# Cross attention of a decoder block on one Trainium2 core: heads taken one unit at a time, or two

## Chip, cores, metric

The kernel runs on one core of one Trainium2 chip. The metric is device time in microseconds (us), median of several executions; lower is better. TensorE (PE in the profile) multiplies into PSUM, VectorE is DVE, ScalarE is ACT, GpSimd is POOL, and SyncE (SP) starts DMAs. Each engine runs its own instructions in the order in which they are written, and semaphores order the engines against each other.

## What is computed

A decoder block over 64 batches of 128 tokens with 128 features: linear attention, cross attention and a mixture of experts, each with a residual and a layer norm. The change is in the cross attention, where the queries come from the latents (the result of the first stage) and keys and values from 120 context rows and the 128 latents together. Cut to what matters:

```
lat = layer_norm(latents); xn = layer_norm(context)
q = lat @ Wq                                   # 16 heads of 64
k, v = split(concat([xn, lat]) @ Wkv)          # 248 keys and values
attn = softmax(q @ k.T / 8)                    # per head, 128 x 248
out = (attn @ v).merge_heads() @ Wout
x = layer_norm(latents + out)
```

## The kernel before

Three stages follow each other: linear_attention (to about 285 us of the span), cross_attention (to about 1,697 us) and experts. `cross_attention` goes through 32 rounds r of two batches. A round has 8 pairs of heads j and 2 batches u, so 16 units s = 2j + u; a unit is two heads of one batch.

The operations of TensorE, with the short names that the text uses (after the PSUM tile that they fill):

- T, four transpositions of a unit's probabilities into `ps_T` (two banks; line 1358). It waits for `prob_ready` of its unit.
- S, the scores of the unit LEAD = 3 ahead, two heads of three matmuls each, into `ps_S` (three banks; `scores`, line 1305, by `split_product`, lines 846 to 848). Three matmuls stand for one product because each operand is split into a high and a low part.
- G, `make_G` (line 1294) into `ps_G`, the folded queries of a pair three pairs ahead: six matmuls, in even units.
- V, `make_V` (line 1301) into `ps_V`, a quarter of the values of a half round ahead: three matmuls, in odd units.
- O, `gang_output` (line 1333), 32 matmuls of probabilities by values for four units, into `ps_O`, in units 4, 8, 12 and, for the round before, 0.
- Once a round: `output` (32 matmuls by Wout into `ps_V`, unit 2), `ranks` (unit 2), `keys` (four transpositions into `ps_V`, unit 4), `slots.turn_rows` (unit 10) and `slots.logits` (unit 11). The last two, with `ranks`, serve the routing for the experts.

A unit's softmax goes through four engines. DVE takes the maxima of the scores (`maxima`, line 1170), ACT the exponentials and their sums (`exponentials`, line 1104, two heads), DVE the reciprocals (`inverse`, line 1176), POOL multiplies (`weights`, line 1026), and then PE may transpose; ACT copies the transposition to SBUF (line 1118) for O.

PSUM tiles with one buffer tie the rest: `ps_V` is used by V, `output` and `keys` in turn. V after `output` waits for `sum_ready`, which DVE raises in `residual` (line 1182) when it has read the bank. V after `keys` waits for `kT_ready`, raised by DVE's `keys` (lines 1140 and 1141). `out_copy` (line 1166) empties `ps_O` and `V_copy` (line 1162) empties `ps_V` after V. `G_hi` (ACT, line 1098) and `G_lo` (DVE, line 1156) read `ps_G`. DVE also has the steps of the routing (`slots.route`), small instructions each of which waits for the one before it, at the units that the tables ROUTE (steps 0 to 16) and ROUTE_LATE (steps 17 to 25) name.

The order on each engine is written out by hand in its `body(r, par)`: for TensorE at line 1342, DVE 1191, ACT 1107, POOL 1029. Before, all four go unit by unit:

```
for s in range(UNITS):
    pe.wait_ge(prob_ready, unit + s + 1)      # T of unit s
    scores((unit + s + LEAD) % BANKS, ...)    # S of unit s + 3
```

## Time and profile before

| what | us |
|---|---|
| median of 3 executions (lowest, highest) | 2102.3 (2101.9, 2102.84) |
| the profiled execution: its time | 2103.97 |
| its span | 2102.1 |
| granted TensorE clock, mean over the span | 0.974 of full speed |
| TensorE busy in the span | 1959.1 (93%) |
| DVE, ACT, POOL busy | 1527.5 (73%), 1259.2 (60%), 1338.7 (64%) |

The span is what the rows of the profile lie in; the time of that execution is 1.9 us longer. Durations come from this one execution. A timeline row has its start, its duration and its operation; matmuls are pipelined, so what one costs in a dense stream is the distance from its start to the next one's start, not its duration.

### The profile page before, as it was taken

What the parts mean: (1) busy time and instruction counts of PE and PEld (TensorE: products, weight loads), DVE (VectorE), ACT (ScalarE), POOL (GpSimd) and SP (SyncE); (2) the same over time, 40 slices, a digit from 0 to 9 for tenths busy, and PEclk for the clock granted to TensorE, in tenths of its full rate; (3) what the DMA queues carried; (4) which work ended last, traced back from release to release, by engine and by line L of the source; (5) the groups of instructions that cost most, each with busy time, mean ns of one, the idle gap of its engine ahead of it and who ended that gap; (6) DMA issues with size and microseconds to landing.
All of it is one profiled execution on the core that took longest, in us unless ns stands there. A gap on an engine that the chain in (4) does not pass through costs nothing. (4 is left out here: it accounts for less than half of the span.)

```text
span 2102.1 us, 47412 instructions
## 1 busy us (share of the span) xinstructions
PE 1959.1 (93%) x15991; PEld 1697.7 (81%) x15991; DVE 1527.5 (73%) x4030; ACT 1259.2 (60%) x3812; POOL 1338.7 (64%) x1475
## 2 busy tenths in 40 slices
PE   6888859999999999999999999999999989999874
PEld 4555448999999999999999999998999877888763
DVE  5999946777777777777777777778777755555554
ACT  4565526666666666666666666666666644444453
POOL 5899937566666666666666666666666664444564
PEclk9999969999999999999999999999999999999976
DMA  5200000000000000000000000001000022322344
GB/s 141 58 18 18 16 25 6 9 14 22 16 17 14 22 15 17 15 18 17 18 15 14 21 17 15 15 21 33 19 15 14 21 60 75 85 73 74 96 141 120
DMA packets 105022, 75.78 MB, mean 36 GB/s; under 512 B 11044, under 2 KB 98676, under 8 KB 104660
## 3 DMA queue, kind: packets, MB, share of 16 engines
q1 hardware_dynamic: 93732, 53.66, 9.4%
q0 software_dynamic: 8640, 17.97, 2.5%
q8 instruction: 135, 2.21, 0.5%
q10 hardware_dynamic: 2416, 1.12, 0.2%
q14 instruction: 99, 0.81, 0.1%
HBM read 40.15 MB, written 32.57 MB: 35 GB/s over the span
## 5 line engine op out<-in xcount | busy, mean ns | idle before, releaser
L1026 POOL TENSOR_TENSOR x_prob<-x_prob,x_inv 128x496 f32<-128x496 f32 x514 | 521.8, 1015 | 464.2 <-DVE x_inv L1176 461.7
L1104 ACT ACTIVATE x_prob<-x_ps_S,x_nmax 128x248 f32<-128x248 f32 x1028 | 472.8, 467 | 225.7 <-DVE x_nmax L1170 223.8
L1170 DVE TENSOR_REDUCE x_nmax<-x_ps_S 128x2 f32<-128x496 f32 x515 | 345.0, 670 | 106.0 <-PE x_ps_S L848 98.2
L1118 ACT COPY x_probT<-x_ps_T 124x512 f32<-124x512 f32 x512 | 300.3, 587 | 166.8 <-PE x_ps_T L1358 164.2
L846 PE MATMUL x_ps_S<-x_kT_lo,x_G_hi 128*128 128x248 f32 x1030 | 328.9, 319 | 0.0
L1358 PE MATMUL x_ps_T<-ident,x_prob 128*124 128x128 f32 x2048 | 319.4, 278 | 7.8 <-POOL x_prob L1026 6.3
L1358 PEld LDWEIGHTS x_ps_T<-ident,x_prob 128*124 128x124 f32 x2048 | 233.5, 140 | 74.0 <-POOL x_prob L1026 30.0
L848 PE MATMUL x_ps_S<-x_kT_hi,x_G_hi 128*128 128x248 f32 x1030 | 286.1, 278 | 0.0
L847 PE MATMUL x_ps_S<-x_kT_hi,x_G_lo 128*128 128x248 f32 x1030 | 286.0, 278 | 0.0
L1328 PE MATMUL x_ps_O<-x_probT,x_V 124*64 124x128 f32 x4096 | 251.9, 276 | 0.4 <-ACT x_probT L1118 0.4
L1585 POOL DMA_INDIRECT sorted_results<-e_y,w_wkv x142 | 145.1, 1022 | 164.9 <-DVE e_y L1717 153.4
L1156 DVE TENSOR_TENSOR x_G_lo<-x_ps_G,x_G_hi 128x512 fp32r<-128x512 f32 x259 | 178.0, 687 | 89.5 <-ACT x_G_hi L1098 89.2
L1328 PEld LDWEIGHTS x_ps_O<-x_probT,x_V 124*64 124x64 f32 x4096 | 221.0, 137 | 18.8 <-issue 5.2
L1104 ACT ACTIVATION_READ_ACCUMULATOR x_prob<-x_ps_S,x_nmax 128x1 f32 x1028 | 206.9, 201 | 0.0
L1098 ACT CAST x_G_hi<-x_ps_G 128x512 fp32r<-128x512 f32 x259 | 152.4, 589 | 80.4 <-PE x_ps_G L848 79.7
L847 PEld LDWEIGHTS x_ps_S<-x_kT_hi,x_G_lo 128*128 128x128 f32 x1030 | 196.0, 190 | 0.0
L846 PEld LDWEIGHTS x_ps_S<-x_kT_lo,x_G_hi 128*128 128x128 f32 x1030 | 195.1, 189 | 0.0
L848 PEld LDWEIGHTS x_ps_S<-x_kT_hi,x_G_hi 128*128 128x128 f32 x1030 | 194.5, 189 | 0.0
L1162 DVE COPY x_V<-x_ps_V 124x512 f32<-124x512 f32 x259 | 175.5, 678 | 7.6 <-PE x_ps_V L848 7.6
L281 POOL DMA_INDIRECT sorted_rows<-w_rows,slots_slot x128 | 132.1, 1032 | 27.9 <-issue 23.5
L846 PE MATMUL x_ps_G<-x_kT_lo,x_M_hi 128*128 128x256 f32 x518 | 146.1, 282 | 0.4 <-DVE x_G_lo L1156 0.4
L847 PE MATMUL x_ps_G<-x_kT_hi,x_M_lo 128*128 128x256 f32 x518 | 146.3, 282 | 0.0
(239 smaller groups left out, 4478.7 us busy)
## 6 DMA issues: line engine op xcount, KB each, us to landing
w_wkv<-sorted_rows SPq DMA_DIRECT2D x142, 66.0 KB
e_back<-sorted_results SPq DMA_DIRECT2D x28, 256.0 KB, 3.7
x_nk<-latents SPq DMA_DIRECT2D x34, 124.0 KB
latents<-lin_nlat SPq DMA_DIRECT2D x32, 128.0 KB, 1.8
turned_rows<-w_rows SPq DMA_DIRECT2D x32, 128.0 KB, 1.7
w_wq<-turned_rows SPq DMA_DIRECT2D x32, 128.0 KB
out_dram<-e_result SPq DMA_DIRECT2D x16, 256.0 KB, 2.8
x_nk<-in_ctx SPq DMA_DIRECT2D x34, 120.0 KB, 2.3
```

What stands on the lines that cost most here:

```text
L846: nc.tensor.matmul(out, stationary[0], moving[1], start=first, stop=False)
L847: nc.tensor.matmul(out, stationary[1], moving[0], start=False, stop=False)
L848: return nc.tensor.matmul(out, stationary[0], moving[0], start=False, stop=last)
L1026: nc.gpsimd.tensor_tensor(prob[:, k], prob[:, k], inv[:, k].unsqueeze(2).broadcast_to([P, 2, K]), ALU.mult).then_inc(prob_ready, 1)
L1098: nc.scalar.copy(G_part[0][:, pair], ps_G[:]).then_inc(G_hi_ready, 1)
L1104: nc.scalar.activation(prob[:, k, h, :], ps_S[:, n % BANKS, h * K:(h + 1) * K], ACT.Exp, bias=nmax[:, k, h:h + 1], accum_out=total[:, k, h ...
L1118: nc.scalar.copy(probT[0:KT, s % (2 * GANG)], ps_T[0:KT, s % 2, :]).then_inc(probT_ready, 1)
L1156: nc.vector.tensor_tensor(G_part[1][:, pair].rearrange("p h u q -> p (h u q)"), ps_G[:], G_part[0][:, pair].bitcast(F32).rearrange("p h u ...
L1162: nc.vector.tensor_copy(V[:, hf, u, tile, :], ps_V[0:KT, :]).then_inc(V_ready, 1)
L1170: nc.vector.tensor_reduce(nmax[:, k, :], ps_S[:, n % BANKS, 0:2 * K].rearrange("p (h k) -> p h k", h=2), AX, ALU.max, negate=True).then_in ...
L1328: last = nc.tensor.matmul(ps_O[h * DH:(h + 1) * DH, k * S:(k + 1) * S], V[:, j // 4, u, tile, (j % 4 * 2 + h) * DH:(j % 4 * 2 + h + 1) * D ...
L1358: last = nc.tensor.transpose(ps_T[0:KT, s % 2, at:at + S], prob[:, s % RINGS, h, tile * KT:(tile + 1) * KT], ident[:])
```

## The change

The 16 units of a round become 8 steps of two units on PE, ACT and DVE; POOL's order stays. A step j of TensorE is now: T of both units 2j and 2j+1, S of units 2j+3 and 2j+4, G, whatever falls in that step (`output`, `keys`, `logits`, then O in even steps, then `ranks`), and V last. `turn_rows` stands ahead of step 5. ACT has: both copies of the transpositions, exponentials of unit 2j+3, G_hi, exponentials of unit 2j+4. DVE has: V_copy, the routing steps of the even unit, inverse of unit 2j+2, maxima of units 2j+3 and 2j+4, inverse of unit 2j+3, out_copy, keys or residual, G_lo, the routing steps of the odd unit. The number of instructions that compute stays. Ahead of the first round ACT does the exponentials of three units, before it did two.

The diff: ACT and DVE whole; of TensorE's part the removed lines are left out, the added ones are all there.

```diff
@@ -1106,25 +1106,25 @@

             def body(r, par):
                 unit = r * UNITS
-                for s in range(UNITS):
-                    exponentials(unit + s + 2, (s + 2) % RINGS)
-                    if s == 10 and r:
+                for j in range(PAIRS):
+                    if j == 5 and r:
                         if r == 1:
                             act.wait_ge(part_ready, 10)
                         slots.turned_rows(act, ps_O, r - 1)
-                    if s == 12 and r:
+                    for s in (2 * j, 2 * j + 1):
+                        act.wait_ge(T_psum, unit + s + 1)
+                        nc.scalar.copy(probT[0:KT, s % (2 * GANG)], ps_T[0:KT, s % 2, :]).then_inc(probT_ready, 1)
+                    if j == 6 and r:
                         slots.scores_of(act, r - 1)
-                    act.wait_ge(T_psum, unit + s + 1)
-                    nc.scalar.copy(probT[0:KT, s % (2 * GANG)], ps_T[0:KT, s % 2, :]).then_inc(probT_ready, 1)
-                    if s % 2 == 0:
-                        ahead = s // 2 + 3
-                        G_hi(r * PAIRS + ahead, ahead % 2)
+                    exponentials(unit + 2 * j + 3, (2 * j + 3) % RINGS)
+                    G_hi(r * PAIRS + j + 3, (j + 3) % 2)
+                    exponentials(unit + 2 * j + 4, (2 * j + 4) % RINGS)

             act.wait_ge(wT_psum, 5)
             nc.scalar.copy(gwT[:], ps_O[:, 0:EXPERTS]).then_inc(wT_ready, 1)
             for j in range(3):
                 G_hi(j, j % 2)
-            for k in range(2):
+            for k in range(3):
                 exponentials(k, k)
             rounds(act, body)

@@ -1190,32 +1190,38 @@

             def body(r, par):
                 unit = r * UNITS
-                for s in range(UNITS):
-                    j = s // 2
-                    if s == 0 and later_round(r):
+                for j in range(PAIRS):
+                    s = 2 * j
+                    if j == 0 and r:
                         V_copy(r * 8 + 3, 0, 1, 1)
-                    if s and s % 2 == 0:
+                    if j:
                         k = j - 1
                         V_copy(r * 8 + 4 + k, 1 - k // 4, k % 4 // 2, k % 2)
-                    if s == 5:
+                    routing(r, s)
+                    inverse(unit + s + 2, (s + 2) % RINGS)
+                    maxima(unit + s + 3, (s + 3) % RINGS)
+                    maxima(unit + s + 4, (s + 4) % RINGS)
+                    inverse(unit + s + 3, (s + 3) % RINGS)
+                    if j % 2 == 0 and (j or r):
+                        out_copy(r * GANGS + j // 2 - 1, (j // 2 - 1) % GANGS)
+                    if j == 2:
                         keys(r + 1)
-                    if s % 2:
-                        G_lo(r * PAIRS + j + 3, (j + 3) % 2)
-                    if s % GANG == 1 and (s > 1 or later_round(r)):
-                        out_copy(r * GANGS + s // GANG - 1, (s // GANG - 1) % GANGS)
-                    if s == 3 and later_round(r):
+                    if j == 1 and r:
                         residual(r - 1)
-                    if r and s in ROUTE:
-                        slots.route(dve, ps_O, r - 1, *ROUTE[s])
-                    if r > 1 and s in ROUTE_LATE:
-                        slots.route(dve, ps_O, r - 2, *ROUTE_LATE[s])
-                    if r == MADE:
-                        for k in (s,) if s < 13 else (s * 2 - 13, s * 2 - 12):
-                            slots.table(dve, 0, k)
-                    maxima(unit + s + LEAD, (s + LEAD) % RINGS)
-                    inverse(unit + s + 2, (s + 2) % RINGS)
-                    if s == 7:
+                    G_lo(r * PAIRS + j + 3, (j + 3) % 2)
+                    if j == 3:
                         context_moments(r + 2, par)
+                    routing(r, s + 1)
+
+            def routing(r, s):
+
+                if r and s in ROUTE:
+                    slots.route(dve, ps_O, r - 1, *ROUTE[s])
+                if r > 1 and s in ROUTE_LATE:
+                    slots.route(dve, ps_O, r - 2, *ROUTE_LATE[s])
+                if r == MADE:
+                    for k in (s,) if s < 13 else (s * 2 - 13, s * 2 - 12):
+                        slots.table(dve, 0, k)

             ROUTE = {11: (0, 2), 13: (2, 6), 14: (6, 11), 15: (11, 17)}
             ROUTE_LATE = {3: (RANK_STEP, SLOT_STEP), 6: (SLOT_STEP, 22), 8: (22, STEPS)}
@@ -1341,61 +1347,58 @@

             def body(r, par):
                 unit = r * UNITS
...
+                for j in range(PAIRS):
+                    first = unit + 2 * j
+                    if j == 5 and r:
                         pe.wait_ge(outT_ready, r * GANGS + 2)
                         slots.turn_rows(pe, ps_O, ident, r - 1)
...
+                    for s in (2 * j, 2 * j + 1):
+                        pe.wait_ge(prob_ready, unit + s + 1)
+                        if unit + s > 1:
+                            pe.wait_ge(probT_ready, unit + s - 1)
+                        for h in range(2):
+                            for tile in range(2):
+                                at = (h * 2 + tile) * S
+                                last = nc.tensor.transpose(ps_T[0:KT, s % 2, at:at + S],
+                                                           prob[:, s % RINGS, h, tile * KT:(tile + 1) * KT], ident[:])
+                        last.then_inc(T_psum, 1)
+                    for s in (2 * j, 2 * j + 1):
+                        ahead = (s + LEAD) // 2
+                        if s % 2:
+                            pe.wait_ge(G_lo_ready, r * PAIRS + ahead + 1)
+                        scores((unit + s + LEAD) % BANKS, (s + LEAD) % 2, par if ahead < PAIRS else 1 - par, ahead % 2)
+
+                    ahead = j + 3
+                    pe.wait_ge(G_lo_ready, r * PAIRS + ahead)
+                    if j == 5:
+                        pe.wait_ge(kT_lo_ready, r + 2)
+                    make_G(ahead % 2, par if ahead < PAIRS else 1 - par, ahead % PAIRS)
+                    if j == 1 and r:
                         pe.wait_ge(V_ready, r * 8 + 5)
                         output(r - 1)
...
+                    if j == 2:
                         pe.wait_ge(V_ready, r * 8 + 4 + 2)
                         keys(r + 1, 1 - par)
...
+                    if j == 5 and r:
+                        slots.logits(pe, ps_O, r - 1)
+                    if j % 2 == 0 and first:
+                        if j == 6 and r:
                             pe.wait_ge(slots.shifted_ready, r)
...
+                        if j == 2 and r > 1:
+                            pe.wait_ge(slots.routed, (r - 2) * STEPS + SLOT_STEP)
+                        gang_output(r * GANGS + j // 2 - 1)
+                    if j == 1 and r > 1:
                         pe.wait_ge(outT_ready, r * GANGS)
                         slots.ranks(pe, ps_O, r - 2)
+                    if j == 1 and r:
+                        pe.wait_ge(sum_ready, r)
+                    elif j == 2:
+                        pe.wait_ge(kT_ready, r + 2)
+                    else:
+                        pe.wait_ge(V_ready, r * 8 + 4 + j)
+                    if j == 4:
+                        pe.wait_ge(kT_lo_ready, r + 2)
+                    make_V(par if j < 4 else 1 - par, 1 - j // 4, j % 4 // 2, j % 2)

             pe.wait_ge(kT_lo_ready, 1)
             for k in range(4):
```

How the order moves, at three places. The first is TensorE in a round's steady part, from one T on; a name is out<-in, and what stands in brackets are the semaphores waited for. Before:

```order
L1358 MATMUL x_ps_T<-ident,x_prob 124x128 [waits x_probT_ready,x_prob_ready]
L1358 MATMUL x_ps_T<-ident,x_prob 124x128 x3
L846 MATMUL x_ps_S<-x_kT_lo,x_G_hi 128x248 [waits x_G_lo_ready]
L847 MATMUL x_ps_S<-x_kT_hi,x_G_lo 128x248
L848 MATMUL x_ps_S<-x_kT_hi,x_G_hi 128x248
L846 MATMUL x_ps_S<-x_kT_lo,x_G_hi 128x248
L847 MATMUL x_ps_S<-x_kT_hi,x_G_lo 128x248
L848 MATMUL x_ps_S<-x_kT_hi,x_G_hi 128x248
L846 MATMUL x_ps_V<-x_wv_lo,x_kT_hi 124x512 [waits x_V_ready]
```

And with the change:

```order
L1362 MATMUL x_ps_T<-ident,x_prob 124x128 [waits x_probT_ready,x_prob_ready]
L1362 MATMUL x_ps_T<-ident,x_prob 124x128 x3
L1362 MATMUL x_ps_T<-ident,x_prob 124x128 [waits x_probT_ready,x_prob_ready]
L1362 MATMUL x_ps_T<-ident,x_prob 124x128 x3
L846 MATMUL x_ps_S<-x_kT_lo,x_G_hi 128x248
L847 MATMUL x_ps_S<-x_kT_hi,x_G_lo 128x248
L848 MATMUL x_ps_S<-x_kT_hi,x_G_hi 128x248
L846 MATMUL x_ps_S<-x_kT_lo,x_G_hi 128x248
L847 MATMUL x_ps_S<-x_kT_hi,x_G_lo 128x248
L848 MATMUL x_ps_S<-x_kT_hi,x_G_hi 128x248
L846 MATMUL x_ps_S<-x_kT_lo,x_G_hi 128x248 [waits x_G_lo_ready]
```

Before, one T is followed by one S and then V or G. Now the T of the next unit stands between a T and the S, and both S follow each other.

The second place is DVE around the copy of the new keys (lines 1140 and 1141), step j = 2. Before:

```order
L1162 COPY x_V<-x_ps_V 124x512
L1170 TENSOR_REDUCE x_nmax<-x_ps_S 128x2
L1176 RECIPROCAL x_inv<-x_total 128x2
L1140 TENSOR_SCALAR x_kT_full<-x_ps_V,w_gain 128x2x120
L1141 TENSOR_SCALAR x_kT_full<-x_ps_V,w_gain 128x2x128
L1156 TENSOR_TENSOR x_G_lo<-x_ps_G,x_G_hi 128x512
L1166 COPY x_outT<-x_ps_O 128x512
```

And with the change:

```order
L1162 COPY x_V<-x_ps_V 124x512
L1176 RECIPROCAL x_inv<-x_total 128x2
L1170 TENSOR_REDUCE x_nmax<-x_ps_S 128x2 x2
L1176 RECIPROCAL x_inv<-x_total 128x2
L1166 COPY x_outT<-x_ps_O 128x512
L1140 TENSOR_SCALAR x_kT_full<-x_ps_V,w_gain 128x2x120
L1141 TENSOR_SCALAR x_kT_full<-x_ps_V,w_gain 128x2x128
L1156 TENSOR_TENSOR x_G_lo<-x_ps_G,x_G_hi 128x512
```

The copy of the keys stood ahead of `out_copy` (line 1166), and now stands behind it.

The third place is DVE around routing steps 6 to 10 (lines 373 to 381), from the end of steps 2 to 5 (line 371), in units 13 and 14. Before:

```order
L371 SCALAR_TENSOR_TENSOR slots_order<-slots_equal,slots_index 128x16
L1170 TENSOR_REDUCE x_nmax<-x_ps_S 128x2
L1176 RECIPROCAL x_inv<-x_total 128x2
L1162 COPY x_V<-x_ps_V 124x512
L373 TENSOR_REDUCE slots_col<-slots_order 128x2
L375 TENSOR_TENSOR slots_chosen<-slots_order,slots_col 128x16
L377 SCALAR_TENSOR_TENSOR slots_rest<-slots_chosen,slots_score 128x16
L379 TENSOR_REDUCE slots_col<-slots_rest 128x2
L381 TENSOR_TENSOR slots_equal<-slots_rest,slots_col 128x16
L1170 TENSOR_REDUCE x_nmax<-x_ps_S 128x2
```

And with the change:

```order
L369 TENSOR_TENSOR slots_equal<-slots_score,slots_col 128x16
L371 SCALAR_TENSOR_TENSOR slots_order<-slots_equal,slots_index 128x16
L1162 COPY x_V<-x_ps_V 124x512
L373 TENSOR_REDUCE slots_col<-slots_order 128x2
L375 TENSOR_TENSOR slots_chosen<-slots_order,slots_col 128x16
L377 SCALAR_TENSOR_TENSOR slots_rest<-slots_chosen,slots_score 128x16
L379 TENSOR_REDUCE slots_col<-slots_rest 128x2
L381 TENSOR_TENSOR slots_equal<-slots_rest,slots_col 128x16
L1176 RECIPROCAL x_inv<-x_total 128x2
L1170 TENSOR_REDUCE x_nmax<-x_ps_S 128x2 x2
L1176 RECIPROCAL x_inv<-x_total 128x2
```

Before, the maxima of one unit stood between the two groups of routing steps. Now both groups and `V_copy` stand ahead of an inverse and the next maxima.

## Rows read from the trace of the kernel before

**Rows 1.** The page, its head: the span.

```profile
span 2102.1 us, 47412 instructions
```

**Rows 2.** Windows: us, busy time (x instructions) by engine, clock, DMA share, GB/s.

```profile
500.00:1400.00 900.00, 898.27 (x8502) 826.65 (x8502) 685.80 (x1873) 599.36 (x1894) 586.74 (x695) 1.00 0.06 17
```

**Rows 3.** One line, L1358: ns min/median/max, first and last start, forms.

```profile
L1358 PE MATMUL x_ps_T<-ident,x_prob x2048: 270/272/421, 318.8 to 1686.0; 128*124 128x128 f32 x187
```

**Rows 4.** Timeline, TensorE, 865 to 869 us: start us, us, operation.

```profile
865.67 0.40 PE L846 MATMUL x_ps_V<-x_wv_lo,x_kT_hi 128*124 128x512 f32 x1
...
866.37 0.60 PE L1358 MATMUL x_ps_T<-ident,x_prob 128*124 128x128 f32 x4
...
866.72 0.36 PE L846 MATMUL x_ps_S<-x_kT_lo,x_G_hi 128*128 128x248 f32 x1
...
867.15 0.28 PE L846 MATMUL x_ps_S<-x_kT_lo,x_G_hi 128*128 128x248 f32 x1
...
867.49 0.28 PE L846 MATMUL x_ps_G<-x_kT_lo,x_M_hi 128*128 128x256 f32 x1
...
868.21 0.60 PE L1358 MATMUL x_ps_T<-ident,x_prob 128*124 128x128 f32 x4
```

**Rows 5.** Timeline, all engines, 881 to 908 us: what is read and overwritten.

```profile
881.29 0.26 PE L326 MATMUL x_ps_O<-slots_picked,slots_ones 128*128 128x24 f32 x1
...
881.58 0.42 DVE L1182 TENSOR_TENSOR slots_hsum<-x_ps_V,X 128x256 f32<-128x256 f32 x1 [2.26 <-PE x_ps_V L1317]
...
885.86 0.53 DVE L1140 TENSOR_SCALAR x_kT_full<-x_ps_V,w_gain 128x240 f32<-128x240 f32 x1 [0.40 <-PE x_ps_V L1263]
...
886.31 0.53 DVE L1141 TENSOR_SCALAR x_kT_full<-x_ps_V,w_gain 128x256 f32<-128x256 f32 x1
...
905.33 1.97 PE L1328 MATMUL x_ps_O<-x_probT,x_V 124*64 124x128 f32 x32
...
907.23 0.66 PE L1358 MATMUL x_ps_T<-ident,x_prob 128*124 128x128 f32 x4
...
907.34 0.69 DVE L1166 COPY x_outT<-x_ps_O 128x512 f32<-128x512 f32 x1 [0.60 <-PE x_ps_O L1328]
```

**Rows 6.** Timeline, all engines, 903 to 905 us: the softmax chain of a unit.

```profile
903.40 0.60 PE L1358 MATMUL x_ps_T<-ident,x_prob 128*124 128x128 f32 x4
...
903.72 0.15 DVE L1176 RECIPROCAL x_inv<-x_total 128x2 f32<-128x2 f32 x1
...
903.84 0.47 ACT L1104 ACTIVATE x_prob<-x_ps_S,x_nmax 128x248 f32<-128x248 f32 x1 [0.48 <-DVE x_nmax L1170]
...
903.96 1.01 POOL L1026 TENSOR_TENSOR x_prob<-x_prob,x_inv 128x496 f32<-128x496 f32 x1 [0.97 <-DVE x_inv L1176]
...
904.65 0.20 ACT L1104 ACTIVATION_READ_ACCUMULATOR x_prob<-x_ps_S,x_nmax 128x1 f32 x1
...
904.73 0.67 DVE L1170 TENSOR_REDUCE x_nmax<-x_ps_S 128x2 f32<-128x496 f32 x1 [0.27 <-PE x_ps_S L848]
```

**Rows 7.** Timeline, VectorE, 866 to 869 us and 907 to 909 us: routing steps.

```profile
867.17 0.16 DVE L373 TENSOR_REDUCE slots_col<-slots_order 128x2 f32<-128x16 f32 x1
...
868.33 0.67 DVE L1170 TENSOR_REDUCE x_nmax<-x_ps_S 128x2 f32<-128x496 f32 x1
...
907.95 0.16 DVE L365 TENSOR_REDUCE slots_col<-slots_score 128x2 f32<-128x16 f32 x1
...
908.66 0.67 DVE L1170 TENSOR_REDUCE x_nmax<-x_ps_S 128x2 f32<-128x496 f32 x1
```

**Rows 8.** Windows, other stages, columns as in rows 2.

```profile
96.00:106.00 10.00, 8.37 (x37) 5.22 (x35) 9.93 (x18) 6.06 (x15) 9.28 (x7) 1.00 0.05 13
...
2001.50:2005.00 3.50, 1.29 (x8) 0.94 (x8) 2.81 (x14) 0.63 (x2) 3.02 (x4) 1.00 0.25 55
...
2005.00:2008.50 3.50, 3.35 (x16) 3.02 (x15) 1.46 (x4) 2.79 (x8) 2.01 (x2) 0.53 0.65 198
```

**Rows 9.** Waits, 500 to 1400 us: us in total, times, longest us.

```profile
PEld x_ps_T L1358 <- POOL x_prob L1026: 15.1, 43, 0.5
```

42 lines of the change are left out of this document (removed).

## The prediction

> **What bounds the kernel now.** I read the windows by stage first, because the change touches one stage only. From 500 to 1400 us, inside the cross attention, TensorE is busy for 898.27 of 900 us at the full clock, while DVE has 686, ACT 599 and POOL 587 us [rows 2]. So TensorE sets the pace, and the other three have slack in total. The stage has 512 units; their transpositions start between 318.8 and 1686.0 us [rows 3], so a unit takes 2.67 us and a round of 16 takes 42.7 us. The waits say how near the softmax chain is: T waited for POOL 43 times in those 900 us, for 15.1 us in all, twice a round at the most [rows 9]. The chain reaches TensorE just in time.
>
> **Price of TensorE's stream**, as distances between starts in a dense piece [rows 4]: V 0.70 us (865.67 to 866.37), T 0.35 (to 866.72), S 0.77 (to 867.49), G 0.72 (to 868.21). The second half of S took 0.34 (867.15 to 867.49), so the first half after a T took 0.43: the switch from a transposition to a product costs some 0.08 us. O took 1.90 (905.33 to the T at 907.23), and DVE reads its result from 907.34 on, 0.11 later [rows 5].
>
> **What the change gains.** Before, each of 16 S of a round follows a T; now 8 do. That is 8 x 0.08 = 0.64 us a round. Whatever else changes neighbours (V after O instead of T after O) I take at nothing, as both are a switch out of the same O; bounds are the 0.08 either way, four times a round, 0.3 us.
>
> **What the change costs: the lead of S over T.** Unit 2j+3 gets its scores in step j and its transposition as the second T of step j+1. Between that T and the one of step j TensorE has only one step of work. The loop closes: the second T releases S in program order, S releases the softmax, the softmax releases the second T of the next step. Its length is read in one place [rows 6]:
> - second T starts at 903.40, its S is ready and the maxima start at 904.73: 1.33 us;
> - maxima 0.67;
> - exponentials with their sums from 903.84 to 904.65 + 0.20: 1.01;
> - reciprocal start to POOL's start, 903.72 to 903.96: 0.24;
> - POOL 1.01;
> - three more handovers (DVE to ACT, ACT to DVE, POOL to PE). The one from DVE to POOL took 0.09 (903.72 + 0.15 to 903.96); most are shorter, and I estimate 0.13 for the three.
>
> Sum 4.39 us. A step without O holds S + S + G + V + T + T = 0.77 + 0.69 + 0.72 + 0.70 + 0.35 + 0.35 = 3.58 us; with the switches rounded less coarsely 3.59. Before, the distance was three units, at least 5.5 us, and covered the chain. Now each short step ends in a wait:
> - step 3: 4.39 - 3.59 = 0.80 us.
> - step 5: it also holds the logits, four matmuls like a T, taken as 0.36: 0.44 us left.
> - step 7: here DVE is late besides. After step 6's O (end at time 0) DVE has out_copy from 0.11, occupying it 0.61 (907.34 to 907.95), G_lo the same, routing steps 2 to 5 0.71 (907.95 to 908.66), V_copy 0.61 (as many elements as out_copy), steps 6 to 10 1.16 (867.17 to 868.33), the inverse 0.08 [rows 5, 7]. The next maxima can start at 3.89. Their S is ready 1.33 after a second T that starts at 0.70 + 0.36 = 1.06, so at 2.39. The chain is 1.50 longer: 4.39 + 1.50 - 3.59 = 2.30 us. The third place in the order shows the cause, the maxima no longer stand between the two groups.
> - steps 0, 2, 4, 6 hold an O, 5.5 us and more, and step 1 `output`, 3.5 us: no wait.
>
> **Two waits for `ps_V`.** In step 2, V stands right behind O and waits for `kT_ready`. DVE does `out_copy` first, and that waits for O's end. From O's end: 0.11, then 0.61, then the two key copies, 885.86 to 886.31 + 0.53 = 0.98, and 0.05 to wake PE: 1.75 us idle [rows 5]. Before, T and S stood between, and the copies ran under O. In step 1, V waits for `sum_ready`: the residual's read started 0.29 us after `output` ended (881.29 to 881.58) and took 0.42 [rows 5]; with the wake-up 0.76, of which `ranks` covers 0.22: 0.54 us. Both have the work that used to hide them behind them now.
>
> **turn_rows** in step 5 waits for the `out_copy` of step 4's O, with only V between: 0.11 + 0.69 - 0.70 = 0.1 at least, more where routing steps 22 to 25 delay DVE; I take 0.3 (bounds 0.1 and 0.6).
>
> **Sum.** Costs 0.80 + 0.44 + 2.30 + 1.75 + 0.54 + 0.30 = 6.13; gains 0.64, and 0.4 of present waits that these replace (15.1 us over 21 rounds is 0.7 on the load side, less in the stream). Net 5.1 us a round. Round 0 has no residual, O or routing and waits for POOL's splitting of weights anyway, so 31 rounds: +158 us. Linear attention and experts don't change.
>
> **The clock.** The waits make TensorE idle for about an eighth of a round, and at the turn of the round nearly without a break: T alone lies between some 0.5 and 1.8 us of idle. In the experts' stage a stretch of 3.5 us with 1.29 us of work at full clock was followed by one at 0.53 of it, 1.2 instead of 2.4 GHz, for 3.5 us; a stretch of the first stage with 8.37 of 10 us busy kept 1.00 [rows 8]. The turn of the round is like the former, the rest like the latter. One such fall costs 3.4/2 = 1.7 us. Between never and each round I take one round in three, as how the idle time falls matters: 0.55 us a round, +17 us. The Trainium skill (TensorE: Matmul & The Clock Gate, Why this matters for your kernels) warns only of idle gaps between bursts longer than any single one expected here; by that rule this term is nothing and the time 2260. The rows above, a fall after a gap of 2.2 us, speak for the term.
>
> The profiled execution took 2103.97 us for a span of 2102.1 [rows 1]. 2104 + 158 + 17 = 2279; it stood 1.7 above the median, so **2278 us**, 8% slower.
>
> **Rivals.**
> - *The chain fits.* If the softmax of a unit took under 3.6 us from T to T, and the two V waits were hidden, only the switches would remain: 2102 - 32 x 0.64 = 2082 us, faster. For it: the mean busy shares of 65 to 76% [rows 2]. Against it: the 4.39 us come from engines that did not queue, and nothing in the change shortens them. It decides at 3.6 us. Chance 0.03.
> - *The chain alone.* DVE's late maxima and the V waits could be shorter than worked out, if DVE gets through its queue faster than these rows say, or if the bank is free earlier than the semaphores' order suggests. With the chain's 0.80 + 0.44 + 0.80 alone: 2.04 - 1.04 = 1.0 a round, 2133 us. Chance 0.05.
> - *The clock falls in each round.* 1.7 instead of 0.55 a round: 2314 us; with a second fall at step 2's 1.75 us wait, 2350. For it: the rows of the experts' stage. Against it: in step 2 dense O and V stand on both sides. Chance 0.17.
> - *Nothing moves*, if the slots were taken up elsewhere. The order on TensorE did change in each round. Chance 0.01.
>
> The forecast has 0.74. The range goes from 2215 to 2325. Below: the V waits, turn_rows and DVE's delay a quarter smaller ((1.75 + 0.54 + 0.30 + 1.50) x 0.25 x 31 = 32 us), no fall of the clock (17) and the chain 0.15 shorter at its three places (14). Above: a fall each round and 10 us. This leaves out the rivals at 2082, 2102 and 2133 and the double fall, under 0.2 in all. A change under 0.2% can't be told from none here. Faster by more 0.03, within it 0.01, slower 0.96.
>
> **What would show it.** In the profile after: PE busy near 88% of a longer cross stage, rounds of about 48 us; DVE, ACT and POOL busy the same in us. Among the waits, T for POOL's `x_prob` grows from 15 us to about 4 us a round, V for the keys and for the residual appear new with 1.7 and 0.5 us. S in second place takes 0.69. If the second T of steps 4, 6 and 0 doesn't wait, the chain is misread; if V of step 2 doesn't wait, the order on DVE isn't what decides; a clock of 0.97 over the stage confirms the one in three.

## The result, and the profile after

| | us | runs | ratio to before, 95% interval |
|---|---|---|---|
| before | 2102.1 | 4, 2099.61 to 2102.84 | |
| after | 2297.36 | 4, 2293.72 to 2299.96 | 1.093, 1.0909 to 1.0951 |

The change makes the kernel 9.3% slower. The prediction was 2278 us in a range of 2215 to 2325. The direction and the range hold; the median lies 19 us above the point.

The page of the kernel after: its head (answers to [rows 1]), TensorE's busy time, and the costliest group of the transpositions (busy us, mean ns of one, idle us before them and the releaser of most of it).

```profile
span 2293.2 us, 47416 instructions
...
PE 2009.0 (88%) x15991; PEld 1722.9 (75%) x15991; DVE 1508.6 (66%) x4030; ACT 1253.0 (55%) x3816; POOL 1339.4 (58%) x1475
...
L1362 PE MATMUL x_ps_T<-ident,x_prob 128*124 128x128 f32 x2048 | 289.4, 276 | 85.5 <-POOL x_prob L1026 81.6
...
L846 PE MATMUL x_ps_V<-x_wv_lo,x_kT_hi 128*124 128x512 f32 x260 | 121.7, 468 | 72.6 <-DVE x_kT_full L1141 53.8
```

DVE, ACT and POOL have nearly the same busy time as before (1508.6, 1253.0 and 1339.4 against 1527.5, 1259.2 and 1338.7 us). The span is 191 us longer, and TensorE is idle in 141 of it (2293.2 less 2009.0 is 284, before 143). Two groups, T and V, hold 158 us of the idle time. TensorE's busy time grew as well, by 50 us for the same work: a matmul at half the clock counts as busy, and a short wait can hide under the duration of the matmul ahead of it (more on that at the last experiment).

Windows of the kernel after, columns as in [rows 2]:

```profile
500.00:1500.00 1000.00, 904.48 (x8260) 819.79 (x8261) 652.94 (x1816) 577.15 (x1840) 570.91 (x673) 0.99 0.05 15
```

Before it was 898.27 of 900 us [rows 2]; now it is 90%. By the starts of T, which go from 319.6 to 1876.7 us here against 318.8 to 1686.0 [rows 3], the median round takes 48.46 instead of 42.80 us, 48.43 where the clock stays up and 49.95 where it doesn't. The waits of TensorE in the same 1000 us (20.6 rounds), load side and stream, answer to [rows 9]:

```profile
PEld x_ps_T L1362 <- POOL x_prob L1026: 77.8, 82, 1.9
...
PE x_ps_T L1362 <- POOL x_prob L1026: 51.4, 62, 1.7
...
PE x_ps_V L846 <- DVE x_kT_full L1141: 33.6, 20, 1.7
...
PE x_ps_V L846 <- DVE slots_hsum L1182: 7.9, 20, 0.4
```

T waits on the load side four times a round for 3.8 us, where it waited twice for 0.7. V waits once a round for the keys and once for the residual, both new.

One round in TensorE's timeline, 1011 to 1049 us (start, duration, operation). A new row begins where another operation does; its start minus the one before it is what that operation took.

```profile
1011.51 0.26 PE L328 MATMUL x_ps_O<-slots_picked,slots_before 128*128 128x16 f32 x1
1012.16 0.49 PE L846 MATMUL x_ps_V<-x_wv_lo,x_kT_hi 128*124 128x512 f32 x1 [0.39 <-DVE slots_hsum L1182]
...
1016.44 1.97 PE L1334 MATMUL x_ps_O<-x_probT,x_V 124*64 124x128 f32 x32
1020.09 0.49 PE L846 MATMUL x_ps_V<-x_wv_lo,x_kT_hi 128*124 128x512 f32 x1 [1.68 <-DVE x_kT_full L1141]
...
1020.89 1.04 PE L1362 MATMUL x_ps_T<-ident,x_prob 128*124 128x128 f32 x8
...
1021.68 0.36 PE L846 MATMUL x_ps_S<-x_kT_lo,x_G_hi 128*128 128x248 f32 x1
...
1023.15 0.28 PE L846 MATMUL x_ps_G<-x_kT_lo,x_M_hi 128*128 128x256 f32 x1
...
1024.56 0.60 PE L1362 MATMUL x_ps_T<-ident,x_prob 128*124 128x128 f32 x4
1025.72 0.65 PE L1362 MATMUL x_ps_T<-ident,x_prob 128*124 128x128 f32 x4 [0.56 <-POOL x_prob L1026]
1026.13 0.36 PE L846 MATMUL x_ps_S<-x_kT_lo,x_G_hi 128*128 128x248 f32 x1
...
1030.29 0.50 PE L846 MATMUL x_ps_V<-x_wv_lo,x_kT_hi 128*124 128x512 f32 x1
...
1031.15 0.44 PE L311 MATMUL x_ps_O<-ident,w_rows 128*128 128x128 f32 x2
...
1035.53 1.39 PE L1362 MATMUL x_ps_T<-ident,x_prob 128*124 128x128 f32 x8
1036.67 0.36 PE L846 MATMUL x_ps_S<-x_kT_lo,x_G_hi 128*128 128x248 f32 x1
...
1040.85 0.50 PE L846 MATMUL x_ps_V<-x_wv_lo,x_kT_hi 128*124 128x512 f32 x1
...
1041.64 1.03 PE L1362 MATMUL x_ps_T<-ident,x_prob 128*124 128x128 f32 x8
...
1044.60 0.40 PE L846 MATMUL x_ps_V<-x_wv_lo,x_kT_hi 128*124 128x512 f32 x1
...
1045.68 0.65 PE L1362 MATMUL x_ps_T<-ident,x_prob 128*124 128x128 f32 x4 [0.22 <-POOL x_prob L1026]
...
1048.02 0.66 PE L1362 MATMUL x_ps_T<-ident,x_prob 128*124 128x128 f32 x4 [1.69 <-POOL x_prob L1026]
1048.43 0.36 PE L846 MATMUL x_ps_S<-x_kT_lo,x_G_hi 128*128 128x248 f32 x1
```

Without a wait, two T take 0.79 us (1020.89 to 1021.68). From there each wait of the round can be read off. They stand where the loop closes: what a short step 3, 5 or 7 lacks shows at the T of step 4, 6 or 0. In the 17 rounds from the fourth to the thirtieth that have no fall of the clock, every one of these distances is the same within 0.02 us, except at the turn, where it varies by up to 0.13.

- Behind step 3: two T take 1.57 (1024.56 to 1026.13), 0.78 too long.
- Behind step 5: 1.14 (1035.53 to 1036.67), 0.35 too long.
- Turn of the round: V takes 1.08 up to the first T (1044.60 to 1045.68) instead of 0.70, and the two T take 2.75 (to 1048.43): 0.38 + 1.96 = 2.34.
- V for the keys: O takes 3.65 (1016.44 to 1020.09) instead of 1.90: 1.75.
- V for the residual: 0.65 from the last of `ranks` (1011.51 to 1012.16), against 0.11 in a later version ("`output` first") where it doesn't wait: 0.54.
- `turn_rows`: the V ahead of it takes 0.86 (1030.29 to 1031.15). A V that stands behind an O and is followed by nothing that waits takes 0.79 (1040.85 to 1041.64), so this wait is 0.06.

The turn of the round on DVE and POOL, the same execution:

```profile
1044.28 0.17 DVE L381 TENSOR_TENSOR slots_equal<-slots_rest,slots_col 128x16 f32<-128x16 f32 x1
1044.37 0.16 DVE L1176 RECIPROCAL x_inv<-x_total 128x2 f32<-128x2 f32 x1
1044.45 1.23 DVE L1170 TENSOR_REDUCE x_nmax<-x_ps_S 128x2 f32<-128x496 f32 x2
1046.17 0.17 DVE L1176 RECIPROCAL x_inv<-x_total 128x2 f32<-128x2 f32 x1 [0.49 <-ACT x_prob L1104]
```

```profile
1044.61 1.01 POOL L1026 TENSOR_TENSOR x_prob<-x_prob,x_inv 128x496 f32<-128x496 f32 x1 [3.18 <-DVE x_inv L1176]
...
1045.80 1.12 POOL L281 DMA_INDIRECT sorted_rows<-w_rows,slots_slot  x1 [0.17 <-issue]
1046.95 1.02 POOL L1026 TENSOR_TENSOR x_prob<-x_prob,x_inv 128x496 f32<-128x496 f32 x1
```

The maxima start 3.60 us after O's end (1040.85 to 1044.45), behind the last routing step. The reciprocal is done at 1046.34, but POOL multiplies only at 1046.95, because the scatter of sorted rows (line 281) stands ahead of it. T follows POOL's end at 1048.02.

The clock in two turns of the round, windows of 3.4 us (the clock is the third number from the right):

```profile
995.60:999.00 3.40, 1.59 (x12) 1.36 (x13) 2.42 (x10) 2.69 (x11) 3.03 (x4) 1.00 0.06 20
999.00:1002.40 3.40, 3.40 (x19) 3.18 (x18) 2.09 (x6) 1.51 (x6) 1.81 (x3) 0.50 0.08 25
...
1045.60:1049.00 3.40, 1.63 (x13) 1.39 (x14) 2.42 (x10) 2.69 (x11) 3.03 (x4) 1.00 0.09 25
1049.00:1052.40 3.40, 3.40 (x48) 3.27 (x46) 2.02 (x6) 2.39 (x9) 1.95 (x3) 1.00 0.06 20
```

Both turns have the same pauses. After the one TensorE runs at 0.50, 1.2 GHz, for 3.4 us and gets 19 matmuls done, after the other at 1.00 and gets 48. Such a fall follows 10 of the 31 turns; all ten start 2.7 to 3.4 us behind the first T of a round.

### The profile page after: what moved, and what is told of

It is laid out like the page before. It is cut to its first block and busy times, and to the rows that moved or that the text cites. A ratio compares the mean times of both kernels' runs of the same rounds, so it can differ in the third digit from the quotient of the medians.

```text
span 2293.2 us, 47416 instructions
## 1 busy us (share of the span) xinstructions
PE 2009.0 (88%) x15991; PEld 1722.9 (75%) x15991; DVE 1508.6 (66%) x4030; ACT 1253.0 (55%) x3816; POOL 1339.4 (58%) x1475
## 5 line engine op out<-in xcount | busy, mean ns | idle before, releaser
L1116 ACT COPY x_probT<-x_ps_T 124x512 f32<-124x512 f32 x512 | 287.1, 593 | 367.1 <-PE x_ps_T L1362 365.0
L1170 DVE TENSOR_REDUCE x_nmax<-x_ps_S 128x2 f32<-128x496 f32 x515 | 337.6, 669 | 86.2 <-PE x_ps_S L848 83.1
L1362 PE MATMUL x_ps_T<-ident,x_prob 128*124 128x128 f32 x2048 | 289.4, 276 | 85.5 <-POOL x_prob L1026 81.6
L846 PE MATMUL x_ps_S<-x_kT_lo,x_G_hi 128*128 128x248 f32 x1030 | 312.1, 303 | 0.0
L848 PE MATMUL x_ps_S<-x_kT_hi,x_G_hi 128*128 128x248 f32 x1030 | 291.1, 283 | 0.0
L1104 ACT ACTIVATION_READ_ACCUMULATOR x_prob<-x_ps_S,x_nmax 128x1 f32 x1030 | 214.3, 208 | 0.0
L1166 DVE COPY x_outT<-x_ps_O 128x512 f32<-128x512 f32 x128 | 88.5, 692 | 183.3 <-PE x_ps_O L1334 183.3
L846 PE MATMUL x_ps_V<-x_wv_lo,x_kT_hi 128*124 128x512 f32 x260 | 121.7, 468 | 72.6 <-DVE x_kT_full L1141 53.8
L1176 DVE RECIPROCAL x_inv<-x_total 128x2 f32<-128x2 f32 x514 | 82.4, 160 | 104.6 <-ACT x_prob L1104 104.6
```

The costliest lines, as they stand in the source:

```text
L846: nc.tensor.matmul(out, stationary[0], moving[1], start=first, stop=False)
L848: return nc.tensor.matmul(out, stationary[0], moving[0], start=False, stop=last)
L1104: nc.scalar.activation(prob[:, k, h, :], ps_S[:, n % BANKS, h * K:(h + 1) * K], ACT.Exp, bias=nmax[:, k, h:h + 1], accum_out=total[:, k, h ...
L1116: nc.scalar.copy(probT[0:KT, s % (2 * GANG)], ps_T[0:KT, s % 2, :]).then_inc(probT_ready, 1)
L1170: nc.vector.tensor_reduce(nmax[:, k, :], ps_S[:, n % BANKS, 0:2 * K].rearrange("p (h k) -> p h k", h=2), AX, ALU.max, negate=True).then_in ...
L1362: last = nc.tensor.transpose(ps_T[0:KT, s % 2, at:at + S], prob[:, s % RINGS, h, tile * KT:(tile + 1) * KT], ident[:])
```

## The experiments

All are edits of the kernel after, but the last and "the other engines' alone", which edit the kernel before. The round is the median distance of T over 16 units in the profiled execution; "falls" are the stretches of 3.4 us at 0.50 in the cross attention, without the one within 5 us of the stage's start that most versions have, before too. Edits move lines, so T is at L1356 to L1366 in their rows.

| version | us (runs) | ratio, 95% interval | round | falls |
|---|---|---|---|---|
| after | 2297.36 (4) | 1.0930, 1.0909 to 1.0951 | 48.43 | 10 |
| keys first | 2252.23 (4) | 1.0716, 1.0698 to 1.0734 | 46.68 | 19 |
| routing steps behind the maxima | 2261.33 (4) | 1.0755, 1.0737 to 1.0773 | 47.73 | 1 |
| `output` first | 2266.78 (4) | 1.0791, 1.0773 to 1.0809 | 47.89 | 3 |
| scatter late | 2262.71 (4) | 1.0769, 1.0751 to 1.0787 | 47.92 | 0 |
| T S T S | 2222.33 (4) | 1.0576, 1.0559 to 1.0594 | 46.64 | 0 |
| the four repairs together | 2172.15 (4) | 1.0330, 1.0313 to 1.0347 | 44.91 | 0 |
| TensorE's order alone | 2736.88 (2) | 1.3017, 1.2969 to 1.3066 | 61.56 | 79 |
| the other engines' alone | 2418.91 (2) | 1.1505, 1.1482 to 1.1528 | 52.07 | 17 |
| repairs and T S T S | 2133.90 (5) | 1.0151, 1.0136 to 1.0165 | 43.80 | 0 |
| and V ahead of O | 2187.05 (5) | 1.0405, 1.0391 to 1.0419 | 45.48 | 0 |
| and steps behind G_lo | 2105.55 (11) | 1.0018, 1.0009 to 1.0027 | 42.92 | 0 |
| before, two waits taken away | 2085.55 (5) | 0.9925, 0.9911 to 0.9939 | 42.30 | 0 |

(The rounds of the first, second and ninth line are of those without a fall. Before: 42.80 and none.)

**Keys first.** In step 2 DVE reads the keys ahead of `out_copy`.

```diff
+                    if j == 2:
+                        keys(r + 1)
                     if j % 2 == 0 and (j or r):
                         out_copy(r * GANGS + j // 2 - 1, (j // 2 - 1) % GANGS)
-                    if j == 2:
-                        keys(r + 1)
```

> The changed kernel, with VectorE's copy of the new keys moved ahead of out_copy in step 2. Theory (out_copy between the transposed keys and kT_ready makes V wait 1.75 us a round behind O): the wait of V for the keys goes to nothing, but 0.35 to 0.4 us of it comes back as a longer wait of the second T in step 4, whose chain the pause had covered. Net -1.35 to -1.45 us a round, 31 rounds: 2297 - 43 = about 2253 us. Rival (V waits because O holds TensorE or the bank, whatever VectorE does first): the wait stays, 2297 us.

Measured: the wait of V for the keys is gone, and the round without a fall is 1.75 us shorter (48.43 to 46.68). The term is confirmed to the hundredth. The 0.35 to 0.4 us that were to come back in step 4 did not: the two T there take 1.59 us, before the edit 1.57. That the time came out at the expected 2253 is luck. The time fell by 45 us and not by 54, because 19 instead of 10 rounds have a fall, though the waits at the turn are the same.

**Routing steps behind the maxima.** In step 7 DVE does the maxima and the inverse first, the steps 6 to 10 behind them.

```diff
-                    routing(r, s)
+                    if j < 7:
+                        routing(r, s)
                     inverse(unit + s + 2, (s + 2) % RINGS)
                     maxima(unit + s + 3, (s + 3) % RINGS)
                     maxima(unit + s + 4, (s + 4) % RINGS)
                     inverse(unit + s + 3, (s + 3) % RINGS)
+                    if j == 7:
+                        routing(r, s)
```

> The changed kernel, with routing steps 6 to 10 of step 7 moved behind the two maxima and the inverse on VectorE. Theory (VectorE is late for the maxima in step 7, so T waits 2.3 us at the turn of the round, and that long pause makes the clock fall in one round of three): the wait at the turn shrinks by 1.0 to 1.1 us, the first of the two T does not wait at all, and the granted clock no longer falls at the turn, 15 us more. 2297 - 32 - 15 = about 2250 us. Rival 1 (the wait is the chain's length alone): unchanged, 2297 us. Rival 2 (the clock falls because of the idle share of the whole round, not of that pause): about 2265 us, with still some 8 to 10 stretches at half clock.

Measured: 0.70 us a round, and the falls nearly gone. 0.70 x 31 = 22 us and nine falls of 1.5 us make the 36 us; the expectation had 47. The steps took 0.91 us in the kernel after (1043.46 to 1044.37 on DVE), and the turn did get 0.90 shorter: V takes 0.70 instead of 1.08 and the two T 2.23 instead of 2.75. But 0.19 came back right behind: the two S of step 0 take 1.65 instead of 1.46, because the moved steps now stand ahead of G_lo, for which the second S waits. One of the steps had become long besides:

```profile
1029.71 1.57 DVE L375 TENSOR_TENSOR slots_chosen<-slots_order,slots_col 128x16 f32<-128x16 f32 x1
```

**`output` first.** In step 1 TensorE does `output` ahead of G, so that G covers the read of the residual.

```diff
+                    if j == 1 and r:
+                        pe.wait_ge(V_ready, r * 8 + 5)
+                        output(r - 1)
                     ahead = j + 3
                     pe.wait_ge(G_lo_ready, r * PAIRS + ahead)
...
                     make_G(ahead % 2, par if ahead < PAIRS else 1 - par, ahead % PAIRS)
-                    if j == 1 and r:
-                        pe.wait_ge(V_ready, r * 8 + 5)
-                        output(r - 1)
```

> The changed kernel, with the output product of step 1 ahead of G. Theory (V in step 1 waits 0.54 us because nothing but ranks stands between output and V): G's 0.7 us cover the residual's read, the wait for the sum goes, nothing takes its place: -0.54 us x 31 = -17 us, 2280 us. Rival (VectorE's residual starts late because it stands behind the second inverse): the wait moves with it, 2297 us.

Measured: 0.54 us a round, as the term said, 17 us. Of the other 14 us of the gain, some 10 come with seven falls fewer, which the expectation of 2280 us did not have; the rest is not accounted for. Taking away half a microsecond some 12 us behind the turn changed how often the turn's pauses bring the clock down.

**Scatter late.** Both of POOL's scatters of a round go behind its last multiplication.

```diff
-                    if s > 13 and r > 1:
-                        slots.scatter(pool, r - 2, 0, s - 14)
+                    if s == 15 and r > 1:
+                        for u in range(2):
+                            slots.scatter(pool, r - 2, 0, u)
```

> The changed kernel, with both scatters of a round's end (POOL's indirect DMAs, 1.1 us each) behind POOL's last multiplication of the round instead of one before it and one behind. Theory (at the turn of the round the inverse is done at 1046.34 us of the changed kernel's trace, and POOL starts the multiplication only at 1046.95, when its scatter ends; so 0.5 of the 2.34 us wait there is POOL's): the wait at the turn shrinks by 0.5 us a round, 2297 - 16 = 2281 us, and down to 2266 if the clock then stops falling. Rival (the multiplication would wait for the inverse and its handover anyway): 2297 us.

Measured: 0.51 us a round and no fall left. So POOL's scatter is a part of the wait at the turn, the one read off POOL's timeline above, and not of the prediction's sum.

**T S T S.** Steps, waits and the other engines stay; only the inner order of TensorE changes back.

```diff
                         last.then_inc(T_psum, 1)
-                    for s in (2 * j, 2 * j + 1):
                         ahead = (s + LEAD) // 2
```

> The changed kernel, with TensorE's four groups of a step in turns, T S T S, as before the change; all the rest stays. Theory A (the loop from one second T over the S behind it to the next second T sets the short steps; and the switch from T to S costs nothing, as T T S S took 2.25 us in the trace, the same as 2 x (0.35 + 0.77)): the S of unit 2j+3 is released by the first T, 0.4 us earlier than its own step's second T, so the waits of steps 3 and 5 (0.78 and 0.35 us) go, and the one at the turn shrinks from 2.3 to about 1.6 us; the outT wait before turn_rows grows by 0.6. Net about -1.1 us a round, 2263 us, less up to 15 where the clock no longer falls. Theory B (as the prediction had it, each change from T to S costs 0.08 us): 0.64 us a round dearer than A, 2283 us; T S T S would then be longer than T T S S by 0.16 us in the trace.

Measured: 75 us less, better than either theory. The waits behind steps 3 and 5 vanish (1.13), that at the turn shrinks from 2.34 to 1.64 (V takes 1.07 instead of 0.70, T S T S 3.52 instead of 2.25), and no fall is left; the other three stay. Theory A missed 26 to 41 us, mostly because it had the wait before `turn_rows` grow by 0.6 us: the V ahead of it takes 0.86 us in both versions. TensorE's timeline of this version, a step without a wait:

```profile
1037.03 0.60 PE L1362 MATMUL x_ps_T<-ident,x_prob 128*124 128x128 f32 x4
...
1037.38 0.36 PE L846 MATMUL x_ps_S<-x_kT_lo,x_G_hi 128*128 128x248 f32 x1
...
1038.16 0.60 PE L1362 MATMUL x_ps_T<-ident,x_prob 128*124 128x128 f32 x4
...
1039.28 0.28 PE L846 MATMUL x_ps_G<-x_kT_lo,x_M_hi 128*128 128x256 f32 x1
```

T S T S takes 2.25 us (1037.03 to 1039.28). T T S S in the kernel after takes 2.26 (1020.89 to 1023.15). There are twice as many changes from T to S, and they cost nothing.

**The four repairs together**: the four diffs ahead of T S T S.

> The changed kernel with four repairs at once: keys ahead of out_copy, routing steps 6 to 10 behind the maxima, output ahead of G, both scatters behind the last multiplication. TensorE's order T T S S stays. Theory (what is left is the loop over the second T, with 0.8 us in step 3, 0.45 in step 5, 0.8 at the turn, and V behind O at 0.05 a time): 2.0 + 0.2 - 0.4 = 1.8 us a round over the kernel before, 2102 + 31 x 1.8 = about 2158 us, no falls of the clock. Rival (the repairs overlap: each hides behind a wait that another one takes away): over 2190 us.

Measured: 14 us more than expected, with 44.91 a round, 2.11 above before. The four repairs took 3.5 us off a round, as much as one by one (1.75 + 0.70 + 0.54 + 0.51), so they don't overlap. The timeline accounts for 2.0 of the 2.11 that are left: 0.77 behind step 3 and 0.35 behind step 5, which no repair touches, 0.91 for T and 0.18 for S at the turn, 0.2 for V behind O (below), less the 0.4 that the present waits of before had. The expectation had 1.8; it took the turn's rest at 0.8 where T and S together have 1.09.

**TensorE's order alone** has TensorE's new block with the old ones of ACT and DVE; **the other engines' alone** has ACT's and DVE's new ones with TensorE's old. In the blocks that are new:

```diff
-                for s in range(UNITS):
+                for j in range(PAIRS):
...
```

> TensorE's new order alone; ScalarE and VectorE keep the order by units of the kernel before. Theory (in that order G_hi and G_lo stand between the exponentials and the inverse of the odd unit, and G comes later in TensorE's new step; the loop over the second T is then longer in every step, also in those with O): waits of 1 to 3.6 us for T in seven of eight steps, 16 us more a round: about 2600 us. Rival (the order on ScalarE and VectorE matters little, as both have slack): like the changed kernel without its wait for the keys, 2250 us.

> The new order on ScalarE and VectorE alone; TensorE keeps the order by units of the kernel before. Theory (VectorE then takes two maxima ahead of one inverse and of G_lo, so TensorE's G waits for G_lo, V for the keys and for the residual): 8 to 9 us more a round, about 2370 us. Rival (TensorE's lead of three units covers any order behind it): 2110 to 2150 us.

Measured: each half alone is far worse than both, with two executions each. Waits of the first from 500 to 1400 us (14.6 rounds):

```profile
PE x_ps_T L1356 <- POOL x_prob L1026: 195.3, 114, 3.1
```

and of the second (17 rounds):

```profile
PE x_ps_V L846 <- DVE x_kT_full L1141: 43.6, 17, 2.6
PE x_ps_G L846 <- DVE x_G_lo L1156: 32.8, 85, 0.6
...
PE x_ps_V L846 <- DVE slots_hsum L1182: 24.1, 17, 1.4
```

With TensorE's order alone T waits in each step for a softmax that, by the order as written, the other engines issue one unit late; 79 falls of some 1.5 us are 119 of its 635 us over before. The expectation of 2600 had no falls; without them, its 16 us a round hold. With the others' order alone T hardly waits, but everything that TensorE wants from DVE one unit earlier is late, for 9.3 us a round where 8 to 9 were expected; 17 falls come on top. The matching of the orders, which the change does, saves over 120 us against either half. It isn't what costs.

**Repairs and T S T S**: the four repairs and the edit of T S T S.

> The four repairs together with the turns T S T S on TensorE. Theory (the step by pairs itself costs nothing and gains nothing; all of its loss is the loop over the second T, VectorE's order, output, and POOL's scatter, and V behind O costs 0.05 us more than T behind O): the 1.9 us of waits for T that were left in the run with four repairs (44.9 us a round) go, so 43.0 to 43.3 us a round, 2108 to 2118 us, at par or half a per cent over the kernel before. Rival (fewer switches between T and S did save 0.6 us a round in T T S S, which is given back now): over 2125 us.

Measured: 2133.9, some 20 above, and as high as the rival has it. One wait remained that the expectation hadn't:

```profile
1014.01 1.02 DVE L375 TENSOR_TENSOR slots_chosen<-slots_order,slots_col 128x16 f32<-128x16 f32 x1
...
1015.58 0.68 DVE L1157 TENSOR_TENSOR x_G_lo<-x_ps_G,x_G_hi 128x512 fp32r<-128x512 f32 x1
```

```profile
1015.06 0.65 PE L1366 MATMUL x_ps_T<-ident,x_prob 128*124 128x128 f32 x4
1016.31 0.38 PE L846 MATMUL x_ps_S<-x_kT_lo,x_G_hi 128*128 128x248 f32 x1 [0.60 <-DVE x_G_lo L1157]
```

The routing steps, moved behind the maxima, now stand ahead of G_lo, for which S waits. My own repair had made a new wait; the version with that repair alone had it already, at 0.19 us.

**And V ahead of O**: on top of that version, V goes ahead of O in steps 0, 4 and 6.

```diff
+                    if j in (0, 4, 6):
+                        pe.wait_ge(V_ready, r * 8 + 4 + j)
...
+                        make_V(par if j < 4 else 1 - par, 1 - j // 4, j % 4 // 2, j % 2)
                     if j % 2 == 0 and first:
...
                         gang_output(r * GANGS + j // 2 - 1)
```

> As the run with the repairs and the turns, and V ahead of O in steps 0, 4 and 6. Theory (the first V behind O takes 0.33 instead of 0.23 us, the first T behind O 0.16 instead of 0.11): 0.05 us less, three times a round, 5 us under the run with the turns: 2103 to 2113 us. Rival (the end of O then stands right ahead of T, out_copy later against turn_rows in step 5): back to par with that run.

Measured: 53 us slower than the version that it edits, where 5 us less were expected. V behind O had been the cover for `out_copy`; without it `turn_rows` waits (500 to 1400 us):

```profile
PE x_ps_O L311 <- DVE x_outT L1167: 15.9, 20, 0.8
```

and T waits again at the turn (8.8 us in 19 times). By the order that is because O ends 0.7 us later, and with it `out_copy` and all that stands behind it on DVE; no run takes this apart. The rival named the right mechanism, but not the size: it had this version at par.

**And steps behind G_lo**: on top of the repairs with T S T S.

```diff
-                    if j == 7:
-                        routing(r, s)
...
                     G_lo(r * PAIRS + j + 3, (j + 3) % 2)
+                    if j == 7:
+                        routing(r, s)
```

> The four repairs with the turns, but steps 6 to 10 of the routing chain issued behind G_lo instead of ahead of it. Theory: in the version with them ahead, the scores of the second unit at the turn of the round waited 0.6 us for G_lo (11.9 us over 20 waits), because those small steps, one of them 1.02 us long beside POOL, stood ahead of it; with them behind, that wait goes: 43.8 less 0.6 to 0.9 gives about 43.0 us a round, and 2134 less some 25 gives about 2108 us. Rival: the chain at the turn has its next member right behind (maxima, inverse, POOL), so that another wait takes its place, and the time stays between 2125 and 2134 us.

Measured: 2105.55 us over 11 runs, 42.92 a round, 0.88 less, and no wait of S for G_lo left. The theory holds. It also refutes the rival of the version that it edits: nothing had to be given back for more changes from T to S. With T S T S, the four repairs and this one the new form is back to 0.2% from before, and no faster.

**Before, two waits taken away.** An edit of the kernel before: `turn_rows` goes behind T of unit 10 and in unit 14 the inverse goes ahead of the maxima.

```diff
-                    if s == 10 and r:
-                        pe.wait_ge(outT_ready, r * GANGS + 2)
-                        slots.turn_rows(pe, ps_O, ident, r - 1)
...
                     last.then_inc(T_psum, 1)
+                    if s == 10 and r:
+                        pe.wait_ge(outT_ready, r * GANGS + 2)
+                        slots.turn_rows(pe, ps_O, ident, r - 1)
...
+                    if s == 14:
+                        inverse(unit + s + 2, (s + 2) % RINGS)
                     maxima(unit + s + LEAD, (s + LEAD) % RINGS)
-                    inverse(unit + s + 2, (s + 2) % RINGS)
+                    if s != 14:
+                        inverse(unit + s + 2, (s + 2) % RINGS)
```

> The kernel before with two small moves: turn_rows behind the T of unit 10 instead of ahead of it, and in unit 14 VectorE's inverse ahead of its maxima. Theory (its rounds still hold a wait of 0.2 us before turn_rows and one of 0.2 before the first T of a round, both seen in the changed kernel's comparison): 0.35 us a round less, 2102 - 11 = 2091 us. Rival (these waits are the softmax chain, and what is taken there comes back in the next unit): 2102 us.

Measured: 2085.55 us, the fastest of all, 0.75% under before. The window and what is left of T's wait for POOL, 500 to 1400 us, against 15.1 us in [rows 9]:

```profile
500.00:1400.00 900.00, 900.00 (x8611) 839.38 (x8609) 686.03 (x1898) 606.84 (x1913) 593.88 (x703) 1.00 0.06 17
```

```profile
PEld x_ps_T L1358 <- POOL x_prob L1026: 5.2, 23, 0.2
```

The busy time of before, 898.27 of 900, looked like the end of what can be had. But in the same 900 us this version records 8611 matmuls and before 8502 [rows 2], and its round is 0.50 us shorter, where 0.35 were expected. Here are the two places in the kernel before, V ahead of `turn_rows` and V at the turn of the round:

```profile
898.20 0.40 PE L846 MATMUL x_ps_V<-x_wv_lo,x_kT_hi 128*124 128x512 f32 x1
...
899.10 0.41 PE L311 MATMUL x_ps_O<-ident,w_rows 128*128 128x128 f32 x2
```

```profile
869.33 0.39 PE L846 MATMUL x_ps_V<-x_wv_lo,x_kT_hi 128*124 128x512 f32 x1
...
870.22 0.65 PE L1358 MATMUL x_ps_T<-ident,x_prob 128*124 128x128 f32 x4
```

V takes 0.90 and 0.89 us up to the next operation, where it takes 0.70 in [rows 4], and these two 0.2 us are in every round. With the two moves both V take 0.70, and the first T behind the turn takes 0.35 instead of 0.41. The busy time doesn't show it because a matmul's row lasts longer than its place in the stream: each of V's three matmuls has a row of 0.40 us and a place of 0.23, so a wait of up to 0.17 leaves no idle time, and of each of these 0.21 us only some 0.04 does, 1.7 us over 21 rounds: just what 898.27 lacks to 900. The distance between starts shows it.

## Why the prediction was right, and where not

The sum, term by term, us a round (measured in the rounds shown above and, for the waits of before, in the last experiment; the clock over the stage):

| term of the prediction | predicted | measured |
|---|---|---|
| behind step 3 | 0.80 | 0.78 |
| behind step 5 | 0.44 | 0.35 |
| step 7, the turn | 2.30 | 2.34 |
| V for the keys | 1.75 | 1.75 |
| V for the residual | 0.54 | 0.54 |
| turn_rows | 0.30 | 0.06 |
| fewer changes from T to S | -0.64 | 0 |
| V behind O | 0 | 0.2 |
| waits of before that these replace | -0.4 | -0.4 |
| sum | 5.1 | 5.62; by the rounds 5.63 |
| the clock | 0.55 | 0.5 (10 falls of 1.5 in 31 rounds) |

**The loop of the second T is as described.** T waits behind the short steps 3, 5 and 7, and not behind those with an O or `output`. T S T S, which lengthens the distance of the loop, takes the two short waits away and 0.7 us of the one at the turn. The 4.39 us put together from engines that did not queue were right within 0.1.

**The steps that failed** are two sizes under "What the change gains". The first is the 0.08 us for the switch from a transposition to a product in "Price of TensorE's stream". It was read as 0.43 against 0.34 for the two halves of S [rows 4]. But eight transpositions take 0.79 us up to the first S: seven distances of 0.11 and one of 0.03. The start that the rows give S lies too close behind the last transposition, so T looked short by about as much as S looked long. The pair was right (0.35 + 0.77), the split wasn't: T takes 0.44 and S 0.69. T T S S and T S T S take the same time, and the 0.64 us a round of gain was never there. Over 31 rounds that is 20 us, about what the point missed.

The second is V behind O, taken at nothing. O to V costs more than O to T: a V behind O takes 0.79 to 0.80 us up to the next operation, against 0.70 (865.67 to 866.37 in [rows 4]); T behind O had 0.05 more than elsewhere. That leaves some 0.05 in each of four places, 0.2 a round. (V behind `ranks` and behind `logits` is as long, 0.80 and 0.78, and T there was longer by the same 0.05.) The bound of 0.3 held it. Against it stood `turn_rows`, whose wait I took at 0.30 and which was 0.06, near the bound of 0.1.

**The turn was right in sum by two parts that were wrong.** I had DVE late by 1.50 us. The maxima start 3.60 after O's end, not 3.89: routing steps 6 to 10 take 0.91 here (1043.46 to 1044.37), not the 1.16 of [rows 7], where one of them, line 375, took 0.40 instead of 0.18. And S is ready at about 1043.4 (second T at 1042.08, and 1.33), so DVE is 1.05 late. The other 0.5 is POOL's scatter ahead of the multiplication: 0.24 after the reciprocal's start, as in [rows 6], POOL could have begun at 1046.41, and it began at 1046.95; I had left POOL's queue out. Scatter late took 0.51 off the round, and routing steps behind the maxima 0.90 off the turn, each by itself, which shows that both are in the chain.

**The clock.** One round in three was the forecast, 10 of 31 it was. The share is partly luck: four small edits that leave the turn's waits alone or shorten them slightly gave 19, 3, 1 and 0 falls. That the falls belong to the turn is shown by where they start, right behind it, and T S T S and scatter late, which shorten its pauses, have none. Which of the turns is struck depends on more than the pauses' length. It isn't random: six of the nine distances between falls are 146.8 us, three rounds, and in the version with keys first they are mostly 47.8 and 95.6 in alternation, one round and two. That points to where in time a turn lies, so that a slightly shorter round changes how many are struck; no run tests it, and it stays open. The Trainium skill (TensorE: Matmul & The Clock Gate, Why this matters for your kernels) warns there only of idle gaps longer than any in these rounds. The trace disagrees: the longest pause here is below 2 us, a T stands between it and a shorter one, and the clock still fell. The sign that I named for one fall in three was wrong: ten falls in the stage leave a mean clock of 0.99, not 0.97.

**The rivals.** "The chain fits" and "nothing moves" are refuted by the waits. "The chain alone" had the V waits hidden; they were there in full. "A fall each round" overrated it by three; its second fall would have cost another 1.7 x 31 = 53 us and made 2367, not 2350.

## What to carry to other kernels

An order by hand has to be checked as a loop: for each operation that waits, how much work of the waiting engine lies between the thing that releases the chain and the thing that needs its end. Two of everything in turn shortens that distance at one place, here from three units of work to two, though nothing is added, and a few instructions moved out of the way of one wait may stand in the way of the next, so look at who waits for what they now precede. And take the price of a sequence from its whole length between two equal places, not from the first start behind a change of operation.
